# Layer outputs of a recommendation tower computed in pairs, in the two banks of one pair of the PSUM ring

## The reference

```
pij = jnp.einsum('bpe,dpe,bpd->bp', p, kernel, q)      # p, q: the pair's two embeddings
z = pij @ W.T + b                                      # 496 -> 256
h = jnp.concatenate([z, dense_ctx], axis=1)            # 272
h = jnp.maximum(h @ W_top1 + b_top1, 0.0)              # 512
h = jnp.maximum(h @ W_top2 + b_top2, 0.0)              # 256
y = h @ W_top3                                         # 1
```

## Time and profile before

| | |
|---|---|
| median of 3 runs | 823.51 us (820.65 to 825.17) |
| the profiled execution | 825.15 us, of which the span is 823.4 us |
| TensorE matmul busy | 772.7 us (94%) |
| VectorE busy | 623.8 us (76%) |
| ScalarE busy | 552.4 us (67%) |
| GpSimd busy | 472.0 us (57%) |
| matmuls of the layers (L747), 28 outputs | 58.6 + 29.3 + 7.5 us busy |

### The profile page before, as it was taken

The page is one execution under the profiler, slowest core; times in us unless marked ns, Lnnn a source line. Parts: engine busy times, 40 slices in busy tenths (PEclk is TensorE's granted clock), DMA queues, the critical chain, the costliest instruction groups (busy, mean ns, idle before and its releaser), DMA issues.

```text
span 823.4 us, 29630 instructions
## 1 busy us (share of the span) xinstructions
PE 772.7 (94%) x11784; PEld 284.5 (35%) x11784; DVE 623.8 (76%) x580; ACT 552.4 (67%) x4181; POOL 472.0 (57%) x502
## 2 busy tenths in 40 slices
PE   4988899999999999989999999998999999998978
PEld 1323233434333333333433333333343333332333
DVE  4487899999755669989866758997885568997930
ACT  0112799999616588999614768999813668999911
POOL 5777777777777777777777777777774000000000
PEclk9999999999999999999999999999999999999999
DMA  9911111111111111111111111111110000000000
GB/s 260 358 41 29 28 30 28 30 29 29 30 30 28 28 29 28 30 29 30 28 31 27 29 28 30 29 30 28 30 30 19 2 2 2 3 3 2 3 3 0
DMA packets 21681, 30.50 MB, mean 37 GB/s; under 512 B 10898, under 2 KB 11410, under 8 KB 20904
## 3 DMA queue, kind: packets, MB, share of 16 engines
q0 software_dynamic: 15872, 16.28, 10.3%
q1 hardware_dynamic: 3512, 9.58, 3.3%
q10 hardware_dynamic: 2160, 2.76, 1.3%
HBM read 28.58 MB, written 0.01 MB: 35 GB/s over the span
## 4 chain that ended last, share of the span: by engine, by line
PE 69%; ACT 11%; POOL 7%; DVE 6%; issue 5%; DMA 2%; SPq 0%; DVEq 0%; POOLq 0%
PE bilinear L679 27%; PE sums L721 14%; PE bilinear L747 11%; PE bilinear L693 10%; ACT batch_prod L505 10%; POOL emb L420 5%; PE bilinear L656 3%; DVE prod L572 3%; PE bilinear L610 2%; POOL emb_first L420 2%; DVE prod L575 2%; DMA sums_sb<-looked_ids 1%; DVE w_comb_sb L555 1%; PE sums L705 1%; DMA emb<-table,ids_sb 1%
## 5 line engine op out<-in xcount | busy, mean ns | idle before, releaser
L505 ACT ACTIVATE batch_prod<-batch_prod 128x64 f32<-128x64 f32 x2048 | 489.6, 243 | 21.2 <-DVE batch_prod L586 21.1
L575 DVE TENSOR_TENSOR prod<-bilinear,emb_t 128x1024 f32<-128x1024 f32 x352 | 415.9, 1218 | 81.4 <-PE bilinear L679 79.8
L420 POOL DMA_INDIRECT emb<-table,ids_sb x368 | 347.3, 944 | 112.1 <-issue 110.3
L505 ACT ACTIVATION_READ_ACCUMULATOR batch_prod<-batch_prod 128x1 f32 x2048 | 387.3, 189 | 0.0
L679 PE MATMUL bilinear<-emb_t,k_sb 64*32 64x512 f32 x5888 | 371.7, 595 | 6.8 <-DVE prod L572 4.8
L721 PE MATMUL sums<-prod,row_sel 64*32 64x512 f32 x2944 | 199.3, 596 | 9.8 <-ACT sums_sb L475 8.1
L586 DVE TENSOR_TENSOR batch_prod<-bilinear,emb_first 128x1024 f32<-128x1024 f32 x128 | 156.1, 1219 | 52.7 <-PE bilinear L693 51.7
L679 PEld LDWEIGHTS bilinear<-emb_t,k_sb 64*32 64x32 f32 x5888 | 108.5, 106 | 204.2 <-issue 137.7
L420 POOL DMA_INDIRECT emb_first<-table,ids_sb x128 | 124.1, 969 | 44.7 <-issue 37.6
L693 PE MATMUL bilinear<-k_sb,emb_t 64*32 64x512 f32 x2048 | 139.9, 601 | 0.0
L464 ACT ACTIVATE emb_t<-bilinear 128x1024 f32<-128x1024 f32 (+1 forms) x40 | 33.9, 848 | 97.8 <-PE bilinear L656 91.2
(11 more groups left out here) (29 smaller groups left out, 105.3 us busy)
## 6 DMA issues: line engine op xcount, KB each, us to landing
emb<-table,ids_sb POOLq DMA_INDIRECT x368, 2.5
emb_first<-table,ids_sb POOLq DMA_INDIRECT x128, 2.5
k_sb<-k_slots SPq DMA_DIRECT2D x2, 896.0 KB, 19.8
k_sb<-k_slots SPq DMA_DIRECT2D x1, 1600.0 KB, 23.1
k_sb<-k_slots SPq DMA_DIRECT2D x1, 1408.0 KB, 19.4
k_sb<-k_slots SPq DMA_DIRECT2D x1, 1088.0 KB, 16.8
sums_sb<-looked_ids SPq DMA_DIRECT2D x1, 1024.0 KB, 9.6
k_sb<-k_slots SPq DMA_DIRECT2D x1, 1024.0 KB, 26.5
```

Source lines behind the costliest of these rows:

```text
L420: nc.gpsimd.indirect_dma_start(fields_of(i, j, t)[:, f % 2, :], None, tables[f], bass.IndirectOffsetOnAxis(ap=ids_sb[:, start + t, f:f + 1 ...
L505: last = nc.scalar.activation(products, products, ACT.Copy, accum_out=batch_sums[:, t, half, row + f:row + f + 1])
L575: last = nc.vector.tensor_tensor(prod[:, at:at + 2, 0:n], bilinear[:, bank:bank + 2, 0:n], emb_t[:, j:j + 1, 0:n].to_broadcast([P, 2, n]), ...
```

## The change

Layers are issued two at a time at slots 10 (k = 0, 1), 18 (k = 2, 3), 26 (k = 4, 5) and 34 (k = 6). A pair takes one use of the ring: the even one writes the first bank of the pair and the odd one the second (`layer_bank`). TensorE waits for a free pair ahead of the even one only, and whoever takes that pair three uses later waits for both copies by ScalarE. The matmuls, ScalarE's copies and all else are the same; at the end of the program the seven still stand one behind another.

```diff
-            if i > 0 and (which - FIRST_LAYER) % LAYER_EVERY == 0 and 0 <= k < NOUTS:
-                steps.append(("layer", i - 1, k))
+            if i > 0 and (which - FIRST_LAYER) % LAYER_EVERY == 0 and 0 <= k < NOUTS and k % 2 == 0:
+
+                steps += [("layer", i - 1, out) for out in range(k, min(k + 2, NOUTS))]
...
-RING_USES = [step for step in PROGRAM if step[0] in ("slot", "batch", "turn", "layer")]
+RING_USES = [step for step in PROGRAM
+             if step[0] in ("slot", "batch", "turn") or (step[0] == "layer" and step[2] % 2 == 0)]
...
+        def layer_bank(i, k):
+            return bilinear[:, ring_bank("layer", i, k - k % 2) + k % 2, :]
...
-                source = bilinear[:, ring_bank("layer", i, k), 0:n]
+                source = layer_bank(i, k)[:, 0:n]
...
-                    pe.wait_ge(s_layer_out, i * NOUTS + which + 1)
+                    pe.wait_ge(s_layer_out, i * NOUTS + min(which + 2, NOUTS))
...
-                ring_free("layer", i, k)
+                if k % 2 == 0:
+                    ring_free("layer", i, k)
...
-                    last = nc.tensor.matmul(bilinear[0:weights.shape[1], ring_bank("layer", i, k), 0:n], weights, x,
+                    last = nc.tensor.matmul(layer_bank(i, k)[0:weights.shape[1], 0:n], weights, x,
```

## The result

The changed kernel takes **816.21 us** (median of 4 runs, 815.36 to 816.45) against 824.18 for the one before (4 runs, 820.65 to 825.17): ratio 0.991, 95% interval 0.989 to 0.994. That is about 8 us, twice the 4.1 that were forecast. The profiled execution took 816.22 us with a span of 814.4, 9.0 us less than before.

The account below looks back on a forecast made before the run. TensorE, busy 94% of the span, was taken as the bound. Visits saved 3.15 us and the fourth layer's stall 1.0, 4.1 in all: 819.4 us from the median of 823.51, range 816.0 to 823.4.

Parts of the forecast that it names:

- The visit at 0.35 us: Each separate layer visit pays 0.35 us entering and leaving whole-array matmuls; 9 visits at slots 14, 22, 30 go: 3.15 us.
- The stall at the fourth layer: Behind slot 22, 1.66 us waiting for slot 21's banks; 1.33 stays, 0.33 goes in each chunk: 1.0 us.
- VectorE keeps up: Over eight slots between visits (10 to 18, 26 to 34), VectorE's multiplies don't delay TensorE: 0 us.
- Rival 1: VectorE becomes the bound in the eight-slot stretches: 0.6 us a chunk, 1.8 in all, 821.2 us; chance 0.12.
- ScalarE: 2.75 us new waiting at paired copies; waits before turns at slots 40 and 54 stay 2.2 and 1.9: value 0.
- Rival 2: ScalarE comes late to turns at slots 40 and 54; wait at sum 32 grows 1.4 a chunk: 823.7 us; chance 0.06.
- Rival 3: The clock falls at the new stall at slot 23: three falls of 1.7 us, 824.5 us; chance 0.06.
- Rival 4: Slot 21's stall goes altogether, spread over sum 9 and the batch: gain 7.7 us, 815.8 us; chance 0.08.
- Moving both together leaves the wait at sum 32 as it is. Value 0: TensorE's 2.52 us wait for ScalarE at sum 32 stays when both layers of the pair at slot 26 move: 0 us.

Follow-up runs that it names:

- one pair alone: Kernel before with k = 3 right behind k = 2 at slot 18, on its own ring use, the visit at slot 22 gone: 819.70 us, ratio 0.995.
- second set: Changed kernel run again without edit beside the kernel before: 816.74 us, ratio 0.991.
- Giving back 1.29 us a chunk: Changed kernel with 1.29 us of repeated matmuls, result overwritten, ahead of k = 0 in each of three chunks: 823.66 us.
- doubling it: Changed kernel with 2.58 us of repeated matmuls ahead of k = 0 in each of three chunks: 824.32 us.
- the run with the order alone: Changed kernel's order of steps, but each layer on its own use of the ring, no shared banks: 815.20 us.

## Why the prediction was right, and by half too small

- **The visit at 0.35 us** was right. The stretches fell by 1.17, 1.42 and 1.37 us for 3 x 0.35 + 0.33 = 1.38; with one pair alone 66.1 to 66.2 became 65.4. The sum took the 1.66 us of chunk 2's stall for all three chunks, though it had read about 1.5 on average. By that reading the term is 3 x (1.5 - 1.33) = 0.5 us in place of 1.0, and the path 3.7, with 3.96 measured: the size of this term was a little lucky.
- **The stall at the fourth layer** was right: it moved to slot 23 at 0.06 us of where the count had it.
- **VectorE keeps up**: right; TensorE waited for it at neither the third nor the last layer. Rival 1 is out, and with it the rule of the Trainium skill (TensorEngine Tiling (Array Packing), PSUM Bottleneck) as the bound of these stretches: the trace shows no wait of that kind there.
- **ScalarE**: right; 2.21 and 1.88 us at the turns, 2.5 at sum 32. Rival 2 is out.
- **Rival 3**, a new fall at the stall at slot 23: no low window stands there in any of the profiles. Rival 4, that slot 21's stall goes, is out by slot 23's wait, though its 815.8 is the number nearest to the result: so far the number was met for a reason that didn't hold.
- **The step that failed** is "Moving both together leaves the wait at sum 32 as it is. Value 0". The wait stayed as it is; its price did not. I had read that price, a low clock behind the stall, and booked it only as something that a new stall might cost. It was 1.70 us a time in each of three chunks, 5.1 us in all that the sum took for fixed, more than the change itself. In the changed kernel one of three stands. That is 3.4 of the missing us, and the fall ahead of chunk 1's first layer is 1.7 more in the profiled pair. The medians' 8.0 and 6.4 us (first and second set) lie above the path's 4.0 by 4.0 and 2.4. No rival had fewer falls than before. That 816.21 stands inside the range at all is luck: its lower end came from the spread of the runs, which have the falls in them, and not from a term for the clock.
- Giving back 1.29 us a chunk brought the falls back and the time of before; doubling it didn't cost another. That the falls depend on when the stalls come, and not on the work, is shown by these doses for the times and the mean clocks, and for the single stalls by the 30 of ten traces. The beat was read from the same traces that it sorts; no run was made to test it, and what sets it stays open.

## What to carry to other kernels

Write the ledger from marks that both kernels share, one stretch at a time: it says at once which part of a difference is in code that was never touched. Before a small change is timed, look for stalls with a low granted clock behind them; each is a loss that may come or go with any shift of the stalls, so either price it into the range on both sides or take the stall away first, as here, where the change was then worth 3.3 us. And look for an engine that waits for another which works through its list in order: here, moving one step in that list by two places was worth 7.6 us to the kernel before, as much as the rebuilt layers with the falls that they happened to miss (8.0 and 6.4), and more than twice what these were worth without.

## What the runs showed of the hardware

Behind a stall of 2.5 us TensorE's granted clock fell to its lower level of 1.2 GHz for a few steps in some executions and not in others, with the stall the same to 0.1 us (2.45 to 2.54); a step of 0.86 us took 1.71 meanwhile (561.26 to 562.97 in the kernel before), and a fall cost 1.70 us. Whether it fell went with when the stall came: the low stretches of one execution begin on one regular beat, and by their place on it 16 stalls with a fall and 14 without are sorted. With stalls 190.9 to 191.3 us apart, a fall was followed by another each of five times. Two layers written to the two banks of one pair, ScalarE reading the first while TensorE wrote the second, took 7.13 us of TensorE's busy time, as did two in different pairs (the run with the order alone).
